# Four pairs in one burst a turn: z, tokens, y of the next four pairs and V ahead of all four products

## What is computed

```python
x = x + _L0_cond_ref(x, L0_cond_W_base, L0_cond_Wt, L0_cond_A, L0_cond_B_w, L0_cond_Wp, L0_cond_scaling, itok_B_0_3)
x = x + _L1_cond_ref(x, L1_cond_W, L1_cond_A, L1_cond_Bm, L1_cond_scalings, itok_B_0_6)
x = x + _L2_cond_ref(x, itok_B_0_7, L2_cond_weights)
x = x + _L3_cond_ref(x, itok_B_1_198, L3_cond_weights)
```

## Time and profile before

| what | us |
|---|---|
| median of 3 runs | 172.35 (172.17 to 172.74) |
| the profiled execution | 172.37 |
| its span | 170.2 |
| PE busy | 163.6 |
| PE's last matmul ends | 167.08 |
| first z of turn 0 starts | 38.51 |

### The profile page before, as it was taken

The page is one execution under the profiler, slowest core; times in us unless marked ns, Lnnn a source line. Parts: engine busy times, 40 slices in busy tenths (PEclk is TensorE's granted clock), DMA queues, the critical chain, the costliest instruction groups (busy, mean ns, idle before and its releaser), DMA issues.

```text
span 170.2 us, 6468 instructions
## 1 busy us (share of the span) xinstructions
PE 163.6 (96%) x2348; PEld 125.0 (73%) x2348; DVE 91.1 (54%) x212; ACT 48.5 (28%) x96; POOL 86.7 (51%) x194
## 2 busy tenths in 40 slices
PE   5889999999999999999999999999999999999992
PEld 5669467678786878687868886877778687868761
DVE  4195975899770846263636645563666180617010
ACT  3142426244230602240223024220503060214021
POOL 4410477764675648475737674756454053608200
PEclk9999999999999999999999999999999999999998
DMA  4799942119550594077309531953394059006406
GB/s 141 252 329 321 282 177 85 33 60 331 190 192 27 168 322 145 23 208 293 131 15 294 209 137 70 285 178 116 123 311 161 31 155 337 2 0 250 123 9 242
DMA packets 16614, 28.75 MB, mean 169 GB/s; under 512 B 3862, under 2 KB 3990, under 8 KB 16598
## 3 DMA queue, kind: packets, MB, share of 16 engines
q1 hardware_dynamic: 14294, 23.31, 41.8%
q0 software_dynamic: 2304, 5.25, 9.1%
HBM read 18.85 MB, written 9.70 MB: 168 GB/s over the span
## 4 chain that ended last, share of the span: by engine, by line
PE 91%; DMA 3%; DVE 1%; SPq 1%; issue 1%; ACT 1%; POOL 0%; DVEq 0%
PE o_ps L751 65%; PE y_ps L751 12%; PE z_ps L751 8%; DMA wb_sb<-in_L_cond_W_base_dram 3%; PE p_ps L751 3%; PE y_ps L764 1%; SPq L231 1%; PE y_ps L811 1%; DVE g L552 0%; PE p_ps L853 0%; DVE b_by L546 0%; ACT o_sb L486 0%; PE p_ps L824 0%; PE z_ps L811 0%; PE p_ps L811 0%
## 5 line engine op out<-in xcount | busy, mean ns | idle before, releaser
L751 PE MATMUL o_ps<-g,yy 128*128 128x512 f32 x384 | 92.1, 395 | 0.0
L751 PEld LDWEIGHTS o_ps<-g,yy 128*128 128x128 f32 x384 | 70.8, 188 | 16.1 <-issue 0.8
L339 POOL COPY u_sel<-u_tab 128x64 f32 x128 | 32.3, 258 | 41.3 <-PE z_ps L751 31.5
L318 POOL DMA_INDIRECT w_all<-in_L_cond_weights_dram,w_rows x32 | 31.8, 994 | 9.6 <-issue 9.6
L631 DVE COPY y_all<-y_ps 128x512 f32<-128x512 f32 x32 | 20.6, 686 | 15.0 <-PE y_ps L751 14.9
L673 DVE COPY o_sb<-o_ps 128x512 f32<-128x512 f32 x15 | 9.7, 687 | 34.5 <-PE o_ps L751 34.5
L426 ACT ACTIVATE yy<-y_all 128x512 fp32r<-128x512 f32 x32 | 19.7, 632 | 16.5 <-DVE y_all L631 16.1
L638 DVE TENSOR_TENSOR yy<-y_all,yy 128x512 fp32r<-128x512 f32 x32 | 21.2, 701 | 3.0 <-ACT yy L426 2.7
L327 POOL DMA_INDIRECT v_sel<-v_table,v_rows x16 | 17.5, 1094 | 6.2 <-issue 6.2
L445 ACT ACTIVATE o_sb<-o_ps 128x512 f32<-128x512 f32 x16 | 8.7, 595 | 37.9 <-PE o_ps L751 37.9
L751 PE MATMUL y_ps<-p_now,x_raw 64*64 64x64 f32 x1024 | 18.6, 221 | 0.0
(11 more groups left out here) (115 smaller groups left out, 104.5 us busy)
## 6 DMA issues: line engine op xcount, KB each, us to landing
x_raw<-in_x_dram SPq DMA_DIRECT2D x16, 512.0 KB, 4.7
out_dram<-o_sb SPq DMA_DIRECT2D x14, 512.0 KB, 5.4
w_sb<-in_L_cond_W_dram SPq DMA_DIRECT2D x4, 256.0 KB, 3.6
wb_sb<-in_L_cond_W_base_dram SPq DMA_DIRECT2D x4, 256.0 KB, 7.1
wp_sb<-in_L_cond_Wp_dram SPq DMA_DIRECT2D x2, 512.0 KB, 6.3
wt_sb<-in_L_cond_Wt_dram SPq DMA_DIRECT2D x1, 1024.0 KB, 8.9
v_table<-v_tab SPq DMA_DIRECT2D x1, 1024.0 KB, 5.7
out_dram<-o_sb SPq DMA_DIRECT2D x4, 256.0 KB, 2.3
```

What stands on the lines that cost most here:

```text
L318: pool.indirect_dma_start(out=w3_all[:, j, :], out_offset=None, in_=w3_flat, in_offset=bass.IndirectOffsetOnAxis(ap=w3_rows[:, j:j + 1], a ...
L339: nc.gpsimd.tensor_copy(u_sel[u][:, :, b, RANK * part:RANK * part + RANK], u_tab[:, :, bass.ds(e, 1), :].rearrange("p k a r -> p k (a r)") ...
L751: return nc.tensor.matmul(dst, lhsT, rhs, start=start, stop=stop)
```

## The change

y now has four banks (all of y_ps); there is no bank for z or p. z of both halves goes to the bank of o_ps[0], tokens to the second bank of y (the last z, and that of turn 0, to y's first bank). y_all and u_sel have four buffers. A turn on PE is: z of half 0, tokens of the next turn, z of half 1, with a wait for p ahead of its last chunk, both mixes of the next turn, V, which now opens the four o banks, then the four products. Each o bank is copied out when its own product is done. Turn 0 is written out: tokens of turns 0 and 1 both lie in the setup, x of turn 1 is loaded into o_sb, and p of turn 1 goes to p_next. In the last turn V stands behind the first product.

In the setup w1 is loaded by column blocks, in turn with w_base's first two, and each block gives one g1_k; the flips, the first products and the third step of g01 move forward, the ids come as single rows on ACT's queue and are spread over the partitions by one matmul; PE's warming matmuls use a blank tile and start before the identity is there.

The diff, cut to its core:

```diff
-        y_ps = ctx.enter_context(nc.psum_tensor("y_ps", [PART, 2, D], F32))
+        y_ps = ctx.enter_context(nc.psum_tensor("y_ps", [PART, QUAD, D], F32))
...
-        z_ps = ctx.enter_context(nc.psum_tensor("z_ps", [PART, D], F32))
-        p_ps = ctx.enter_context(nc.psum_tensor("p_ps", [PART, D], F32))
...
@@ -205,7 +209,16 @@

         def y_of(u):

-            return y_ps[:, :, D // 2 * (u % 2):D // 2 * (u % 2) + D // 2].rearrange("p b (k t) -> p b k t", k=KC)
+            at = D // 2 * (u % 2)
+            return y_ps[:, u // 2 * 2:u // 2 * 2 + 2, at:at + D // 2].rearrange("p b (k t) -> p b k t", k=KC)
+
+        def p_bank(i):
+
+            at = D // 2 if isinstance(i, int) and i == 1 else 0
+            return y_ps[:, 1, at:at + QUAD * SEQ]
...
-            w1_rows = w1.rearrange("(c p) d -> p c d", p=PART)
+            w1_rows = w1.rearrange("(c p) (k d) -> p k c d", p=PART, d=PART)
...
-            for c in range(KC):
-                sp.dma_start(w1_sb[:, c, :], w1_rows[:, c, :]).then_inc(w1_in[c], 16)
-            for k in range(2):
-                load_wb(k)
-            sp.dma_start(ids[:, 2, :], e3_ids.partition_broadcast(PART)).then_inc(e3_in, 16)
-            for n, t in enumerate((e0_ids, e1_ids, e2_ids)):
-                sp.dma_start(code_ids[:, n, :], t.partition_broadcast(1)).then_inc(code_in, 16)
+            for k in range(KC):
+                sp.dma_start(w1_sb[:, k, :, :], w1_rows[:, k, :, :]).then_inc(w1_in[k], 16)
+                if k < 2:
+                    load_wb(k)
...
-            sp.dma_start(s0_sb[:, :], s0.partition_broadcast(PART)).then_inc(b0_in, 16)
-            sp.dma_start(b0_sb[:, :, :, :], b0.rearrange("e (p s) r -> p e s r", s=KC)).then_inc(b0_in, 16)
+            load_wb(2)
...
+            sp.dma_start(s0_sb[:, :], s0.partition_broadcast(PART)).then_inc(b0_in, 16)
+            sp.dma_start(b0_sb[:, :, :, :], b0.rearrange("e (p s) r -> p e s r", s=KC)).then_inc(b0_in, 16)
             sp.dma_start(wt_sb[:, :, :], w_t.rearrange("(c p) d -> p c d", p=PART)).then_inc(wt_in, 16)
-            for k in range(2, KC):
-                load_wb(k)
+            load_wb(3)
...
-            for n, t in enumerate((e0_ids, e1_ids)):
-                sp.dma_start(ids[:, n, :], t.partition_broadcast(PART)).then_inc(ids_in, 16)
...
+                sp.dma_start(o_sb[:, 2 * h:2 * h + 2, :], x_rows[:, QUAD + 2 * h:QUAD + 2 * h + 2, :]).then_inc(x_next_in[h], 16)
...
-            load(1, 0)
-            load(1, 1)
-            load(2, 0)
-
-            def turn(i, loads=2):
-                for h in range(2):
-                    store(i - 1, h)
-                    if loads > h:
-                        load(i + 1 + h, 1 - h)
+            for h in (1, 0):
+                load(2, h)
+            store(0, 0)
+
+            def turn(i, more=True):
+                store(i - 1, 1)
+                if more:
+                    for h in (1, 0):
+                        load(i + 2, h)
+                store(i, 0)
...
+            for k in range(KC):
+                pool.wait_ge(w1_in[k], 16)
+                blk = w1_sb[:, k, k, :]
                 nc.gpsimd.tensor_tensor(blk, blk, ident[:, :], ALU.add).then_inc(w1_plus, 1)
-            for k in range(2):
-                plus_wb(k)
-            for k in range(2, KC):
-                plus_wb(k)
+                if k < 2:
+                    plus_wb(k)
             pool.wait_ge(rows_set, 1)
-            gather_w3(range(0, W3_FIRST - 1))
+            gather_w3(range(0, 1))
+            plus_wb(2)
+            gather_w3(range(1, 5))
+            plus_wb(3)
+            gather_w3(range(5, W3_FIRST - 1))
...
-            place_u(0, 0)
+            for h in range(2):
+                place_u(0, h)
...
+            def gather_turn(i):
                 first = W3_FIRST + W3_TURN * i
                 if first < PAIRS:
                     wait(pool, w3_more, 16 * W3_TURN * i)
-                    gather_w3(range(first, first + 1))
-                if i < QUADS - 1:
-                    pool.wait_ge(z_done, 2 * i + 2)
-                    place_u(i + 1, 0)
-                    if first < PAIRS:
-                        pool.wait_ge(y_done, QUAD * (i + 1) + 2)
-                        gather_w3(range(first + 1, first + W3_TURN))
+                    gather_w3(range(first, first + W3_TURN))
+
+            pool.wait_ge(z_done, 1)
+            place_u(1, 0)
+            pool.wait_ge(y_done, 2 * QUAD)
+            pool.wait_ge(table_out, 32)
+            pool.wait_ge(v_rows_set, 4)
+            fetch_v(0)
+            gather_turn(0)
+            place_u(1, 1)
+            fetch_v(1)
+            for i in range(1, QUADS - 1):
+                pool.wait_ge(z_done, i + 1)
+                place_u(i + 1, 0)
+                fetch_v(i + 1)
+                gather_turn(i)
+                place_u(i + 1, 1)
...
+            for n, t in enumerate((e0_ids, e1_ids, e2_ids, e3_ids)):
+                act.dma_start(ids_row[:, n, :], t.partition_broadcast(1)).then_inc(ids_in, 16)
...
+            def turn(i, more=True):
+                if more:
+                    copy_p(i + 1)
+                high_y(i, 3)
+                copy_z(i, o_ps[0] if more else y_ps[:, 0, :])
+                if more:
+                    high_y(i + 1, 0)
+                    copy_out(i, 0)
+                    high_y(i + 1, 1)
+                    copy_out(i, 2)
+                    high_y(i + 1, 2)
+
+            for i in range(2):
+                copy_p(i)
...
+            for u in range(2):
+                high_y(0, u)
+            copy_z(0, y_ps[:, 0, :])
+            for u in range(2, QUAD):
+                high_y(0, u)
+            for u in range(3):
+                high_y(1, u)
+            for u in (0, 2):
+                copy_out(0, u, by=2 * QUAD)
...
+            low_g1(0)
+            dve.wait_ge(ids_in, 64)
+            nc.vector.tensor_copy(ids_f[:, :, :], ids_row[:, :, :]).then_inc(ids_f_set, 1)
+            low_g1(1)
             low_wb(1)
-            for k in range(2, KC):
-                low_g1(k)
+            dve.wait_ge(ids_spread, 1)
+            nc.vector.tensor_copy(ids[:, :, :].rearrange("p n b -> p (n b)"), y_ps[:, 3, 0:4 * BATCH]).then_inc(ids_set, 1)
+            dve.wait_ge(ids_set, 1)
             find_w3_rows()
-            scale(E0, b0_in, b0_sb, b0_now, s0_sb)
-            dve.wait_ge(code_in, 48)
-            link(nc.vector.scalar_tensor_tensor(out=code_part[:, 0, :], in0=code_ids[:, 1, :], scalar=float(E0),
-                                                in1=code_ids[:, 0, :], op0=ALU.mult, op1=ALU.add))
+            low_g1(2)
...
+            def turn(i, ahead=True, more=True):
+                copy_out(i - 1, 3)
+                low_y(i, 3)
+                if more:
+                    for u in (2, 3, 0, 1):
+                        copy_y(i + 1, u)
                 if ahead:
                     place_w2(i + 2)
+                    add_w3(i + 2)
                 if more:
-                    pass_y(i + 1, 0)
-                if ahead:
-                    add_w3(i + 2)
+                    low_y(i + 1, 0)
+                    copy_out(i, 1)
+                    low_y(i + 1, 1)
+                    low_y(i + 1, 2)

             dve.wait_ge(setup_dve, DVE_DONE["w2T"])
             dve.wait_ge(code_set, 1)
             place_w2(0)
+            place_w2(1, w2_next)
...
-            place_w2(1, w2_next)
+            add_w3(1, w3_next)
+            find_v_rows()
             dve.wait_ge(setup_act, ACT_DONE["v0g1"])
             read("v0g1", v0g1[0:R0, :], bank_of("v0g1")[0:R0, :], v0g1_low[:, :], ALU.add)
-            add_w3(1, w3_next)
-            find_v_rows()
             dve.wait_ge(setup_act, ACT_DONE["v0g1_both"])
-            for g in (2, 1, 0, 3):
+            for g in (1, 3, 0, 2):
...
-            for u in range(2):
+            for u in (2, 3, 0, 1):
                 copy_y(0, u)
             low_g01(0)
             low_y(0, 0)
             for k in range(1, KC):
                 low_g01(k)
-            low_y(0, 1)
-            turn(0, first=True)
+            for u in range(1, QUAD):
+                low_y(0, u)
+            for u in (2, 3, 0, 1):
+                copy_y(1, u)
+            place_w2(2)
+            add_w3(2)
+            for u in range(3):
+                low_y(1, u)
+            copy_out(0, 1, by=2 * QUAD)
...
+            pe.wait_ge(blank_set, 1)
+            keep_warm(18)
             pe.wait_ge(ident_set, 1)
-            keep_warm(16)
-            for c in range(KC):
...
+                last.then_inc(setup_ps, 1)
+
+            flip_w1(0)
+            keep_warm(6)
+            g01_high()
+            flip_w1(1)
             g01_step(0)
+            pe.wait_ge(ids_f_set, 2)
+            mm(y_ps[:, 3, 0:4 * BATCH], ones_row[:, :], ids_f[:, :, :].rearrange("p n b -> p (n b)"),
+               True, True).then_inc(ids_spread, 1)
+            flip_w1(2)
             g01_step(1)
+            pe.wait_ge(ids_set, 1)
```

(90 more changed lines are left out.)

248 lines of the change are left out of this document (96 added, 152 removed), and 2 rows, old and new, of the table ORDER.

## The result

The changed kernel takes 186.78 us (median of six runs, 186.26 to 189.08) against 172.73 us for the kernel before on the same chip: ratio 1.082 (1.078 to 1.086). The profiled run took 186.26 us with a span of 184.4. The forecast was 173.0 with a range to 174.5: the direction is right, the size wrong by 13.8 us, or by 13.3 for the profiled run.

A forecast was written before the change was run, and what follows sets the result against it. PE bounds the kernel, busy 163.6 of 170.2 us. Turns -0.45, setup start -1.1, moved setup steps +2.05 and a change of shape +0.1 give +0.6 on 172.37: 173.0 us, range 170.9 to 174.5.

The forecast's parts named there:

- Start of setup, -1.1: Setup up to the flips of wp: w1 by column block lets them begin at 13.8 instead of 14.88, -1.1 us.
- So g1_0 is high at 5.7 in the best case: Setup start: w1's first load at 3.6 to 4.1, POOL's sum 0.5, four flips 0.5, ACT's read 0.6.
- Setup, moved steps, +2.05: Setup: moved work loses covers, so waits of 0.6 before tokens 1, 0.8 before the first mix, 0.55 before z.
- Rival C: Setup: GpSimd and DVE late; with slow w1 loads v1 waits, up to 0.6 more waiting, 174.3 us; chance 0.18.
- Turn 0, 15.46: Turn 0 on PE: both z, two mixes, 36 products, V and 12 products sum to 15.46 us, without a wait for p.
- Loop turn, 15.97 + 0.30: Each loop turn: PE's work 15.97 us plus 0.30 idle for p ahead of z's last quarter, 16.27 in all.
- Rival B: Loop turns: p's copy is hidden, so none waits; 6 x 0.30 = 1.8 us off, 171.2 us; chance 0.22.
- Turn 1, as the others: Turn 1, counted as one of the six loop turns: 16.27 us, with no extra wait.
- POOL's margin: Loop turn: POOL's fetches, gathers and copies end at 14.7, 1.6 us before the next z needs u; stays hidden.

The follow-up runs named there:

- old warming: Changed kernel with 16 identity transposes for the 18 blank matmuls and no second warming: 180.35 us, ratio 0.998 to the kernel before; later runs 1.003, 1.009, 0.997.
- a short warming: Changed kernel, no second warming, warmed by 9 blank matmuls (181.99 us, ratio 1.011), 9 of the identity (177.54, 1.029) or 5 wide blank ones (176.73, 1.026).
- an edit: On the changed kernel with old warming, next turn's tokens moved behind the first quarter of z's first half: 177.92 us, ratio 0.988 to the kernel before.
- the 173.90 us kernel: Changed kernel with old warming, loop tokens behind z's first quarter, turn 1's tokens behind v0g1: 173.90 us, ratio 1.012 to the kernel before.

## Why the prediction was wrong, step by step

- **Start of setup, -1.1.** The failed step. "So g1_0 is high at 5.7 in the best case": the sum chains w1's load, POOL, four flips and ACT as if PE were free, and holds none of the 18 + 6 float32 matmuls that stand around those flips. They are 48 records, 10 us, and the full level came only at 15.15, 3 us into the products (2.1 and 4.2 us in the other two traces). In place of -1.1 it was +6.0. With the old warming the flips of wp came at 14.1 to 14.4 in seven traces, against 13.8: there the rest of the step was right to 0.6 us. In the other four, with the late rise, they came at 16.0 to 16.4; that too the sum had at nothing.
- **Setup, moved steps, +2.05.** Right in kind and size. Waits forecast 0.6, 0.8 and 0.55; measured with the old or a short warming 0.45 (tokens 1), 0.65 (first mix), 0.51 (z), and 0.24 ahead of v and 0.35 ahead of v1 that I had not named: 2.2, of which 0.22, ahead of v1, stood in the kernel before as well. In the changed kernel's first trace the last is 0.16, since the pause gave DVE time.
- **Rival C.** POOL and DVE are late by little: 0.36 us ahead of v1, where the kernel before waits 0.22. It stood for 174.3 and is next to nothing of the miss.
- **Turn 0, 15.46.** Right where PE had its program and its clock (15.43), 16.47 in the first trace (half level until 52.7), 16.9 to 17.8 with the pause.
- **Loop turn, 15.97 + 0.30.** 15.96 + 0.32. Rival B, that the copy of p is hidden, did not hold; by an edit it does.
- **Turn 1, as the others.** 19.56. POOL's margin was named as the thin one: V's rows came 0.41 us late in turn 1, and in no other turn. The 1.72 and what follows it are the program's block.
- **PE's program as free.** No step of the forecast priced it. It is worth 1.55 + 2.7 us in the first trace (with what V lost behind it), perhaps beside some of the clock's 1.3. That the half level from 49.3 to 52.7 comes from the pause isn't shown: with as long a pause, the 173.90 us kernel has no dip.

The sum: 7.1 (warming and clock at the start) + 1.55 (pause) + 0.4 (half level and the rest ahead of z) + 1.0 (half level in turn 0) + 3.3 (turn 1) = 13.4 of 13.3 us.

## What to carry to other kernels

Price warming matmuls as any others, by their own records: a float32 matmul is two, and if it runs while the first data has already landed it is on the path. Look at the distance of the first products, and not at the clock column alone, to see whether the warming raised the clock at all, and look in more than one trace: 16 transposes did it early in seven of eleven, 18 float32 matmuls of a blank tile in none of four. And when many small matmuls are put in one burst ahead of or early in a loop, count instructions as well as time: where 256 of them were used up in 2.0 us TensorE waited for its own program in every trace. At 3.3 to 3.6 us two traces have no pause, and others have one of 0.3 to 1.1. The place moves with every instruction added before it.

## What the runs showed of the hardware that I had not expected

- 36 records of blank matmuls over 7.7 us did not bring TensorE to its full level in four traces: what came next, from 8.88 on, still ran at half the pace. With 16 transposes over 3.5 us the full level came at 4.9 to 6.6 in seven traces of the changed kernel's variants, with nothing but transposes before it, and at 10.5 to 11.3 in four. The profile's clock column reads 1.00 ahead of the rise in all of them.
- A float32 matmul of 128x128 weights and 64 columns takes as long (two records of 0.21 us each, by the flips behind them at the half level) as one with 128 columns.
- TensorE paused 0.3 to 1.9 us at records 338, 466 (128 further on) and 843, each time until 1.2 to 1.6 us after the end of a 16 KB packet of an instruction queue, and never in the loop's later turns.
- Four of six chips ran the kernel before in about 180 us and not 172.5, at the same granted clock in the loop, with 3 to 4.5 us lost in the setup. What makes that is open.
- An idle time of 3.67 us of PE on such a chip was followed at once by 3.4 us at the half level, products 0.43 apart (busy table by stretch, old warming):

```profile
26.00:29.50 3.50, 0.01 (x1) 0.04 (x1) 0.88 (x6) 0.60 (x1) 0.95 (x1) 1.00 0.06 19
29.60:33.00 3.40, 3.40 (x11) 2.71 (x11) 1.76 (x6) 0.39 (x1) 0.00 (x0) 0.50 0.84 296
```
